# A gated cross-attention and mixture-of-experts layer: batch 0's tokens dealt one step sooner, nine transfers inside attention, batch 1 counted in the last step

## What is computed

```python
x = x + tanh(g_xattn[0]) * attention(layernorm(x), ctx, pos)     # 32 heads of 8, axial rope, softmax over 256 keys
x = x + tanh(g_ffn[0]) * ffn(layernorm(x))

def ffn(x):                                                      # 1024 tokens
    shared = sum(relu(flat @ sw1[e] + sb1[e]) @ sw2[e] + sb2[e] for e in range(2)) / 2
    probs  = softmax(flat @ router_w + router_b)                 # 32 experts
    p, i   = top_k(probs, 6);  p = p / p.sum(-1)
    routed = sum(gates[:, e] * (relu(flat @ rw1[e] + rb1[e]) @ rw2[e] + rb2[e]) for e in range(32))
    return shared + routed                                       # hidden width 176
```

## Time and profile before

| | |
|---|---|
| median of 3 runs | 386.52 us (385.31 to 387.3) |
| the profiled execution | 385.19 us, of which the span of the profile is 383.4 us |
| mean granted TensorE clock | 0.948 of full speed |
| busy: PE, DVE, ACT, POOL | 335.2, 238.1, 214.6, 228.4 us |

### The profile page before, as it was taken

How to read it: one execution, slowest core, us unless ns; L and a number is a source line. 1 busy time by engine, 2 the same in 40 slices (tenths; PEclk the granted TensorE clock), 3 DMA queues, 4 the chain that set the end, 5 groups by cost and what they waited for, 6 DMA issues and landing times.

```text
span 383.4 us, 8623 instructions
## 1 busy us (share of the span) xinstructions
PE 335.2 (87%) x2574; PEld 263.5 (69%) x2574; DVE 238.1 (62%) x747; ACT 214.6 (56%) x539; POOL 228.4 (60%) x277
## 2 busy tenths in 40 slices
PE   7879999999999998669775999999999999999900
PEld 5567766666666575436553899999999999999700
DVE  7997788878788787683521355555555555545426
ACT  4795899979879778311312455555555555555400
POOL 8466332105025357777774288888788788787830
PEclk9999999999999899985989899999999999999965
DMA  7699999997005113622324578888888888887688
GB/s 225 209 309 310 308 324 316 321 240 209 11 2 125 27 46 103 228 88 105 115 103 131 131 126 142 132 156 143 142 143 145 142 142 146 136 145 113 71 201 279
DMA packets 63295, 62.20 MB, mean 162 GB/s; under 512 B 6258, under 2 KB 61588, under 8 KB 63252
## 3 DMA queue, kind: packets, MB, share of 16 engines
q1 hardware_dynamic: 48532, 44.60, 39.9%
q0 software_dynamic: 13680, 17.05, 27.6%
q10 hardware_dynamic: 1040, 0.01, 0.2%
HBM read 29.01 MB, written 32.63 MB: 161 GB/s over the span
## 4 chain that ended last, share of the span: by engine, by line
PE 52%; POOL 12%; DVE 11%; DMA 10%; issue 7%; ACT 6%; SPq 0%; POOLq 0%; DVEq 0%
PE psum L1631 14%; PE psum L1613 10%; POOL rows_by_block L521 8%; DMA sum<-ob,xs 7%; PE psum L1324 5%; PE psum L1371 5%; DVE nmax L936 4%; PE psum L1604 4%; PE psum L1622 3%; ACT probs L649 2%; POOL sum L570 2%; PE psum L1219 2%; PE psum L1305 1%; PE psum L1342 1%; DMA w<-sum 1%
## 5 line engine op out<-in xcount | busy, mean ns | idle before, releaser
L570 POOL DMA_INDIRECT sum<-ob,xs x79 | 122.4, 1549 | 39.3 <-DVE ob L1189 28.9
L936 DVE TENSOR_REDUCE nmax<-psum 128x2 f32<-128x512 f32 x128 | 80.3, 683 | 13.0 <-PE psum L1324 12.3
L1631 PE MATMUL psum<-w,hT 88*128 (+1 forms) x316 | 81.5, 380 | 0.0
L649 ACT ACTIVATE probs<-psum 128x512 f32<-128x512 f32 x128 | 69.7, 600 | 14.0 <-PE psum L1342 12.7
L1189 DVE TENSOR_SCALAR ob<-psum,gate 128x256 f32<-128x256 f32 x79 | 38.2, 484 | 50.2 <-PE psum L1631 42.7
L785 ACT ACTIVATE hT<-psum,b1b 88x128 f32<-88x128 f32 x158 | 48.8, 357 | 35.2 <-PE psum L1622 34.7
L1613 PE MATMUL psum<-w,xT 128*128 x316 | 61.4, 317 | 0.3 <-issue 0.3
L1631 PEld LDWEIGHTS psum<-w,hT 88*128 88x128 f32 (+1 forms) x316 | 53.8, 190 | 4.6 <-issue 0.3
L521 POOL DMA_INDIRECT rows_by_block<-Vx,slot x48 | 47.2, 983 | 14.3 <-issue 13.4
L776 ACT ACTIVATE xT<-psum 128x256 f32<-128x256 f32 x79 | 30.3, 384 | 41.8 <-PE psum L1604 41.8
L1613 PEld LDWEIGHTS psum<-w,xT 128*128 128x128 f32 x316 | 48.3, 193 | 1.0 <-issue 0.9
(11 more groups left out here) (199 smaller groups left out, 473.9 us busy)
## 6 DMA issues: line engine op xcount, KB each, us to landing
rows_by_block<-blank SPq DMA_DIRECT2D x1, 10744.0 KB, 38.2
xs<-rows_by_block SPq DMA_DIRECT2D x79, 136.0 KB, 2.6
w<-in_L_ffn_rw_dram SPq DMA_DIRECT2D x2, 2816.0 KB, 22.2
w<-in_L_ffn_rw_dram SPq DMA_DIRECT2D x16, 352.0 KB
sum<-blank SPq DMA_DIRECT2D x3, 1152.0 KB, 13.5
w<-sum SPq DMA_DIRECT2D x12, 256.0 KB, 5.6
sum<-ob,xs POOLq DMA_INDIRECT x79, 4.0
x_sb<-in_x_dram SPq DMA_DIRECT2D x4, 256.0 KB, 3.8
```

What stands on the lines that cost most here:

```text
L570: pool.indirect_dma_start(yd[i], bass.IndirectOffsetOnAxis(ap=xs[b % ROWS_AHEAD][:, X_ID:X_ID + 1].bitcast(U32), axis=0), ob[i][:, :], Non ...
L649: act.activation(probs[g % 2][:, :, n, :], st_bank(g, n)[:, :].rearrange("p (t q) -> p t q", t=TB), ACT.Exp, scale=SCALE).then_inc(exp_ok, 1)
L936: dve.tensor_reduce(nmax[i % 2][:, :, n], S_BANK[(4 * i + n) % SB][:, :].rearrange("p (t k) -> p t k", t=TB), AX.X, ALU.max, negate=True). ...
L1631: ins = pe.matmul(Y_BANK[b % 2][:, 0:D], hT[b % 2][0:rows, c, :], w2[0:rows, bass.ds(expert[b], 1), c, :].rearrange("p a n -> p (a n)"), s ...
```

## The change

Three groups of edits; no operation's size changes.

- **Attention.** Batch 0's row transposes move from step 19 to 18, its router scores from 20 to 19, its counts from 24 to 22, with what hangs on them on ACT, POOL and DVE. Batch 1's output projection moves from steps 22 and 23 to 23 and 24, its scales on POOL from group 24 to 25. `scales` no longer ends with a `row_early`; both row normalisations of a batch stand in the group behind. In POOL's loop the transfers come last in a group. DEALT_AT starts in group 27 and has nine transfers.
- **End of attention.** Batch 1's counts move into step 31, and ACT copies them out of PSUM (`counts_copied`), so `places(1)` works from the copy. The second tile of batch 2's output projection moves from step 31 behind the loop, after a wait for that copy. DVE's loop is one step shorter, and what stood in its last step follows `places(1)`.
- **Behind attention.** On POOL: five transfers, batch 2's root, two transfers, the memsets, six transfers, batch 3's root, the rest. On DVE: batch 3's residual and statistics come ahead of batch 2's gate sums and places; two `shared_sum` come ahead of batch 3's scores, and its places ahead of its gate sums. On PE and ACT: another order of the sibling, where a tile's transpose stands ahead of the product of the tile before, and two tiles' products stand ahead of batch 3's row transposes; counts of batch 2 come behind the last output projection.

The diff, cut to its core:

```diff
-        PROJ_STEPS = {NG * (b + 1) + 6 + t: (b, t) for b in range(B - 1) for t in range(TB)}
-        ROWS_STEPS = {NG * b + 19: b for b in range(EARLY)}
-        SCORE_STEPS = {NG * b + 20: b for b in range(EARLY)}
-        COUNT_STEPS = {24: 0}
+        PROJ_AT = [14, 23, 30]
+        PROJ_STEPS = {14: (0, 0), 15: (0, 1), 23: (1, 0), 24: (1, 1), 30: (2, 0)}
+        ROWS_AT = [18, 27]
+        ROWS_STEPS = {v: b for b, v in enumerate(ROWS_AT)}
+        SCORE_STEPS = {v + 1: b for b, v in enumerate(ROWS_AT)}
+        COUNT_AT = [22, 31]
+        COUNT_STEPS = {v: b for b, v in enumerate(COUNT_AT)}
...
-                row_early(TB * b)
...
-            DEALT_AT = {28: (0, 2), 29: (2, 3), 30: (3, 4), 31: (4, 6)}
+            DEALT_AT = {27: (0, 2), 28: (2, 4), 29: (4, 6), 30: (6, 7), 31: (7, 9)}
+            SCALES_AT = [16, 25]
...
+                for b in range(EARLY):
+                    if g == SCALES_AT[b]:
+                        scales(b)
+                    if g == SCALES_AT[b] + 1:
+                        row_early(TB * b)
+                        row_early(TB * b + 1)
+                    if g == ROWS_AT[b] + 2:
+                        marks_of(b)
+                    if g == ROWS_AT[b] + 3:
+                        mask_early(b)
+                if g == COUNT_AT[0] + 1:
+                    blocks_needed(0)
+                if g == COUNT_AT[0] + 2:
+                    places_early(0)
                 if g in DEALT_AT:
                     deal(*DEALT_AT[g])
-                for b in range(EARLY):
-                    if g == NG * b + 16:
-                        scales(b)
-                    if g == NG * b + 17:
-                        row_early(TB * b + 1)
-                    if g == NG * b + 21:
-                        marks_of(b)
-                    if g == NG * b + 22:
-                        mask_early(b)
-                if g == 25:
-                    blocks_needed(0)
-                if g == 26:
-                    places_early(0)
-
-            deal(DEALT_AT[31][1], DEALT_AT[31][1] + 1)
+
+            deal(DEALT_AT[31][1], EACH + 2)
             inverse_root(EARLY + 4, slice(TB * EARLY, TB * EARLY + TB))
-            deal(DEALT_AT[31][1] + 1, EACH + EACH // 2)
+            deal(EACH + 2, EACH + 4)
...
-            deal(EACH + EACH // 2, EACH + EACH // 2 + 3)
+            deal(EACH + 4, EACH + 10)
             inverse_root(B + 3, slice(NT - TB, NT))
-            deal(EACH + EACH // 2 + 3, NT * TOPK)
+            deal(EACH + 10, NT * TOPK)
...
+            counts_copied(EARLY - 1)
             exponentials(GROUPS - 3, 2)
...
             shared_relu(0)
+            shared_relu(1)
             shared_rows(2)
+            shared_relu(2)
+            shared_rows(3)
             second_rows(B - 1)
-            shared_relu(1)
-            shared_rows(3)
+            shared_relu(3)
+            shared_rows(4)
             gate_exponentials(B - 1)
-            shared_relu(2)
             for n in range(4, NT):
-                shared_rows(n)
-                shared_relu(n - 1)
-            shared_relu(NT - 1)
+                shared_relu(n)
+                if n + 1 < NT:
+                    shared_rows(n + 1)
...
-                if (i, part) == (26, 1):
+                if (i, part) == (24, 3):
                     dve.wait_ge(had_ok, 1)
                     block_ends(0, blocks[:, 0, :]).then_inc(upto_ok, 1)
-                if (i, part) == (27, 3):
+                if (i, part) == (26, 0):
                     dve.wait_ge(placed_ok, 1)
                     slots(0)
-            for i in range(GROUPS + 2):
+            for i in range(GROUPS + 1):
...
             dve.wait_ge(masks_ok, 1)
             places(1)
+            normalise(PAIRS - 3)
+            residual(B - 2, TB - 1)
+            row_statistics(B - 2, TB - 1)
+            variances(TB * EARLY, TB)
             inverse_deviations(TB * EARLY, TB, EARLY + 4)
...
             choose(B - 2)
-            gate_sums(B - 2)
-            places(B - 2)
             for t in range(TB):
                 residual(B - 1, t)
                 row_statistics(B - 1, t)
             variances(3 * TB, TB)
+            gate_sums(B - 2)
+            places(B - 2)
             inverse_deviations(3 * TB, TB, B + 3)
             normalised_rows(B - 1)
+            dve.wait_ge(gfh_ok, 1)
+            shared_sum(0)
+            shared_sum(1)
             scores(B - 1)
             choose(B - 1)
-            dve.wait_ge(gfh_ok, 1)
-            shared_sum(0)
+            places(B - 1)
             gate_sums(B - 1)
-            places(B - 1)
-            shared_sum(1)
+            shared_sum(2)
+            shared_sum(3)
             experts_of_blocks()
...
             pairs(*(shifted_score(GROUPS - 2, n) for n in range(GH)))
+            pe.wait_ge(rk_ok, EARLY)
+            output_projection(B - 2, TB - 1)
             values(GROUPS - 3)
-            counts(1)
...
             shared_transposed(0)
-            counts(B - 2)
             for t in range(TB):
                 output_projection(B - 1, t)
+            counts(B - 2)
             shared_out(0)
+            shared_transposed(1)
             shared_hidden(2)
+            shared_out(1)
+            shared_transposed(2)
+            shared_hidden(3)
             second_rows_transposed(B - 1)
-            shared_transposed(1)
+            shared_transposed(3)
             router_scores(B - 1)
-            shared_out(1)
-            shared_hidden(3)
-            shared_transposed(2)
-            counts(B - 1)
             shared_out(2)
             shared_hidden(4)
-            shared_transposed(3)
+            counts(B - 1)
+            shared_transposed(4)
             shared_out(3)
             shared_hidden(5)
-            shared_transposed(4)
+            shared_transposed(5)
+            shared_out(4)
+            shared_hidden(6)
```

53 lines of the change are left out of this document (30 added, 23 removed).

## The result

| | before | changed |
|---|---|---|
| median of 20 runs | 387.17 us (384.89 to 391.94) | 382.86 us (379.67 to 385.99) |
| the profiled execution | 385.19 us, span 383.4 | 379.67 us, span 377.9 |
| mean granted TensorE clock | 0.948 | 0.955 |

The ratio is 0.9885, with a 95% interval of 0.9861 to 0.9910: faster by 4.4 us, between 3.5 and 5.4. The forecast was 381.4, its range 379.2 to 385.0.

A forecast was written before the change was run, and what follows sets the result against it. What the change can move was taken as bound by POOL's transfers into rows_by_block, the sibling next. From 385.19 us: -2.9 - 3.8 - 0.2 + 1.4 + 0.4 = -5.1, so 380.1 profiled, 381.4 median; range 379.2 to 385.0.

The forecast's parts named there:

- Part 1: Attention, batch 0 a step sooner: DVE's stall on POOL and the slow clock behind it go, 2.9 us gained.
- M: Time of the last pair of maxima in attention, 146.88 us before; forecast to come 2.9 us sooner, at 144.0.
- the ceiling of 3.1: Attention's largest possible gain in us: 1.58 of DVE's stall plus 1.5 for the slow clock behind it.
- Part 2: Nine transfers instead of six before the train behind attention, at no cost: three pitches of 1.275, 3.8 us gained.
- Part 3: Batch 1 counted in step 31: ACT's copy and PE's wait on it cost nothing (bound 0.5 us); nobody waits.
- Part 4: Batches 2 and 3 behind attention: 25th transfer waits for slots, 0.3 us at full clock, 3.2 at half; 1.4 taken.
- The -0.2 of the sum: Behind attention, a wait of POOL on veps (batch 3's residual statistics) falls away, 0.2 us gained.
- Part 5: Shared expert ends near M + 49, off the path by 5 us or more; slow clock at first blocks costs 0.4.
- (a): Attention gives nothing back: stall moves to the row normalisations of groups 17 and 26, clock falls; 384.3 us, chance 0.15.
- (b): PE at half clock from the gap behind attention on, batch 3's slots late; slower, 388.8 us, chance 0.09.
- (c): Shared expert, not the transfers, ends last ahead of the blocks, at 205.3: 382.1 us, chance 0.08.
- (d): Shared-port rule: moved transfers hold up attention's maxima, 3 x 0.7 us: 383.5 us, chance 0.06.

## Why the prediction was right, and where its steps were off

The time lay within 1.5 us of the forecast and the sign was right. Of the 1.46, 0.65 is the start: the sum began from a median of three executions (386.52), and that of twenty is 387.17. The change itself was forecast at -5.1 and measured at -4.4. By its steps:

**Part 1, attention: the stall's price was wrong, and its tie to the clock isn't shown.** DVE has no wait on POOL left in attention, and the granted clock is 1.00 from 84 to 144 us, as said. The 0.2 for the row normalisations was right (PE waits 0.17 at 128.66). M moved by 1.81, not 2.9. The groups tell where: from group 25's cast to group 28's 12.01 us went before and 10.41 now, so 1.60 of the ceiling of 3.1; all other groups together give 0.2.

The sum had booked two things: DVE's stall of 1.58 at its full length, and 1.5 for the slow clock behind it. The run with nine transfers and nothing else has the stall and not the slow clock, and takes 10.71 us for these groups (132.85 - 122.14). So the slow clock had cost 1.30 (12.01 - 10.71), nearly what was booked, and the stall, with whatever the moved steps cost or gave, 0.30 (10.71 - 10.41) instead of 1.58. PE's timeline of the kernel before shows why the stall was cheap:

```profile
125.85 0.38 PE L1324 MATMUL psum<-QK 32*128 32x256 f32 x1 [0.70 <-DVE nmax L936]
```

PE runs ahead of DVE's maxima, so of the 1.58 only 0.70 reached it, and less than half of that reached M. The row with 0.70 stood in the trace of before; I hadn't looked for it. A stall has to be read on the engine that sets the pace, not on the one that stands, and even there it is a ceiling.

The gain of the slow clock is also not safely the change's. The forecast had it under the condition that the stall caused the fall, and with the same stall the clock stayed full once. In the changed kernel's attention it fell in two of twelve profiles, in both of the old attention. Two profiles of the old attention are too few to say whether the change makes the fall rarer.

**Part 2, nine transfers: 3 pitches of 1.27, at no cost to M.** Right in the changed kernel. Seven of them lie before M and two directly behind, before the change four and two, so three pitches leave the train; with six inside, M is the same within 0.25. What I had wrong is the independence: alone this edit is worth nothing (0.9964 to 1.0047), since there the transfers stood ahead of POOL's marks and of batch 1's slots.

**Part 3, batch 1's count at nothing: right as a cost, wrong as a value.** In the kernel with nine inside that lacks it the 13th transfer stands 1.97 us.

**Part 4, the stand at the 25th transfer.** DVE and PE of the changed kernel, the chain to batch 2's slots:

```profile
155.35 0.16 DVE L868 TENSOR_TENSOR newton<-rough 128x2 f32<-128x2 f32 x1 [3.51 <-POOL rough L395]
...
169.39 0.55 DVE L1029 TENSOR_REDUCE slot<-Vx 128x12 uint32<-128x384 f32 x1
```

```profile
157.71 0.41 PE L1401 MATMUL psum<-ident,oT 128*128 128x128 f32 x2 [2.67 <-DVE attn L961]
...
159.57 0.97 PE L1465 MATMUL psum<-rtw_sb,attn 128*128 128x32 f32 x8
```

Forecast and found, behind M: outputs 12.4 and 12.64, end of the router scores 15.25 and 15.47, slots 25.0 and 24.87, POOL's want 24.8 and 24.9. The lower end of 0.3 left out what lies between DVE's end and POOL's start (169.94 to 170.73), 0.8 us; part of that was made up because the sum took 21.6 for the train's stretch where its own row gives 21.84. The profile's stand is 0.75, at full clock. Whether PE's clock falls after the 2.7 us of waiting was the open question of the step, and I took 1.4 as a value between. The answer is that both happen. In the profiled execution it held; in the median execution the loss seems larger: closing the wait gained 2.5 us and filling it 2.9. The profile alone would have shown only the cheap case. Of those 2.9 the trace in which the clock did fall accounts for 1.84 (201.78 - 199.94), by a stand at batch 3's root and a longer one at the 25th transfer; where the other 1.1 lies is open, with the difference of two intervals some 0.5% wide about it. The -0.2 of the sum, POOL's wait at batch 3's root, came true in the profile (0.27 before, none now) and fails whenever the clock falls here: 1.00, 1.59 and, with the old order, 4.11 us in the three traces with a fall.

Batch 3's slots came at M + 39.2, between 37 and 41.5; the clock was at its lower level in part of that stretch (0.79 and 0.53 below), and the 37th transfer starts 1.8 us behind them, 1.0 more than the 0.8 it needs. Windows of the changed kernel:

```profile
170.00:175.00 5.00, 2.57 (x14) 2.23 (x15) 2.68 (x13) 1.39 (x5) 3.35 (x4) 0.79 0.28 105
175.00:180.00 5.00, 5.00 (x12) 3.54 (x13) 2.54 (x11) 0.00 (x0) 3.78 (x5) 0.53 0.25 93
```

**Part 5, the sibling and the block start.** PE and, in the windows, the first blocks:

```profile
193.23 2.76 PE L1570 MATMUL psum<-w2s,Vx 128*128 128x256 f32 x12
204.70 1.09 PE L1628 MATMUL psum<-ident,xs 128*128 128x128 f32 x4 [8.71 <-DMA xs<-rows_by_block]
```

```profile
205.00:210.00 5.00, 4.75 (x19) 4.09 (x18) 0.82 (x4) 1.50 (x5) 0.00 (x0) 0.50 0.85 253
```

The sibling is done at 196.0, M + 50.9 (forecast 49), and no longer the bound, 3.9 us ahead of the last transfer (forecast 5 or more). ACT's first rectified tile has no wait for the memsets. Against the 0.66 of before the clock is 0.50, and the blocks cost 0.56 more (forecast 0.4). The remark that even the old order would end at 205 was wrong in the one trace of it: there the sibling ends at 209.3, and the train, held up by the same order and a low clock, is ready at the same time. In the time the new order is worth 1.3 us, within the intervals, so that it is what lets the train's gain through is likely and not shown.

**The rivals.** (a) fell with M at 145.07 and a clock of 1.00. (b), half clock from the gap on, is real in its first half: three of five profiles have it. But the cost stayed far below what would give the rival's 388.8. In the new order the clock was back before batch 3's rows, and batch 3 held up the 37th transfer in two traces only: with the old order, by 0.58 us (0.88 against 0.30), and with eight idle products, by 0.71 after the later fall from 172.9 to 183.2. (c) fell in the changed kernel; the old order is near it, with the train late as well. (d), the port rule of the Trainium skill (SBUF — State Buffer, "SBUF: two separate sides"), did not show: the transfers in attention took 0.96 to 1.01 us, except 1.25 once, the first, as before, and with eleven inside M stays where it was. DVE's maxima beside them read PSUM; whether any operation beside a transfer held the shared port no run shows, so the rival fell and the rule itself wasn't put to the test.

So part of the agreement is luck. In the profile, 0.4 below the forecast, attention gave 1.1 too little, the stretch from M to the last transfer 0.8 more than booked (3.40 against 3.8 + 0.2 - 1.4 = 2.6), of which 0.65 is the smaller stand, and the tail, which the change doesn't touch, happened to be 0.94 shorter; without it the profile would lie 0.5 above. In the median, 1.5 above, the known parts don't close: 1.1 from attention, some 1.5 from the stand (2.9 against 1.4) and 0.65 from the start make more than the 1.5 found, and no run says what gave the difference back.

## What to carry to other kernels

Where an engine stalls that isn't the one that sets the pace, take the idle time of the pacing engine as the ceiling, and look for its row: 1.58 us of DVE's standing were 0.70 of PE's and 0.30 of the time. Where the clock was low behind a stall, look at a second trace before booking it as the stall's: it may be low in one execution and full in the next. Moves that use up one stretch of free time are worth little alone: ask for each what is the next thing that it waits for, and test it alone. A wait of two to three microseconds on TensorE in a serial stretch can have a second price that one profile may not show; read more than one execution, close the wait, or fill it with work whose length was measured first, and end it before the data is there.

## What the runs showed of the hardware

- A product of the fp32 identity (128 by 128) with itself is two MATMUL records and takes 0.23 to 0.24 us behind attention (20 in 4.63, 8 in 1.95) and 0.26 to 0.27 ahead of the blocks (28 in 7.38, 60 in 16.47). I had taken them for shorter at first: overrunning cost 4 to 5 us by the ratios in the two kernels with sixty (against the same kernels without), and 3.6 in the one with twenty (against eight).
- The granted clock is not fixed by the program: the same instructions with the same 2.7 us of waiting gave 1.00 in one execution and half in another. In attention it fell at 135.4 in two of twelve profiles, PE being busy without a break in the 5 us before, and at 128.5 in one of two executions of the same program. One such fall inside attention costs 1.3 us of the time. The Trainium skill (TensorE: Matmul & The Clock Gate, "Part 1") has idling lower the clock and sustained work restore it; the profiles behind attention agree in the direction, and show the gap of 2 to 2.7 us to be one at which either outcome comes; the two falls in attention at 135.4 and 135.6 came with no idling directly ahead of them.
- An indirect transfer that had to wait for DVE's slots starts 0.79 to 0.80 us after DVE's end (seven cases, 169.94 to 170.73 in the changed kernel for one).
